# Two masks moved: the first attention's mask maximum and row scale later in VectorE's order, the second attention's mask as a 49th row of its key and query stacks

## The chip, the cores and the metric

One Trainium2 chip, one core of it. The metric is the time of one execution of the whole kernel on the device, in microseconds (us). The engines are named as in the profile: PE is TensorE's matmul side and PEld its weight load, DVE is VectorE, ACT is ScalarE, POOL is GpSimd, SP is SyncE, whose queue issues most transfers.

## The reference

The kernel runs two transformer-like layers over x (4 batches of 256 tokens, 256 wide) with a context of 1601 tokens per batch and a mask over the context for each attention. Cut to what matters:

```python
x = x + xattn0(layernorm(x), ctx, mask_b)    # 1 head, 256 wide, softmax over 1601 keys
x = x + ffn0(layernorm(x), ...)              # 16 experts, 6 per token, and 2 shared
x = x + xattn1(layernorm(x), ctx, mask_i, Wq, bq, Wk, bk, Wv, bv, Wo, bo, ...)  # 16 heads of 16
x = x + ffn1(layernorm(x), ...)              # 16 experts, 2 per token, and 1 shared

# xattn0: scores = q @ ctx.T / 16; masked keys to -1e30; softmax; times ctx;
#         the whole result is zero where a batch has no key left (valid)
# xattn1: scores = q @ k.T / 4, clipped to -50..50; masked keys to -10000, clipped again to -50;
#         softmax; times v; projected, scaled, layer norm, gamma and beta
```

## The kernel before

Tokens lie in tiles of 128, so a batch is two tiles and there are eight in all; the 1601 keys are 13 tiles of 128 (the last of 65). fp32 products are made from a rounded high part and a low remainder in three matmuls (`mm3`, lines 657 to 659): hi x hi, lo x hi and hi x lo.

**First attention and projections (stage A).** A loop over i = 0 to 7 (a batch b = i // 2 and one of its two query tiles) runs on PE, ACT and DVE, each with its own order of work written out by hand and counted semaphores between them. In each i PE makes the scores in four pieces (`scores`, two PSUM banks in turn, piece x waits for the evacuation of piece x - 2), two pieces of the key projection, the readout of the query tile before, transposes of the probabilities between two more pieces of the key projection, and four pieces of the value projection. DVE adds the mask to each score piece and takes its maximum (`row_max`), ACT makes the exponential over all 1601 keys, then rounds keys (`kev`, kh), probabilities (`pth`) and the context in natural layout (`nat_hi`, cNh), and DVE makes the low parts (`klo`, `ptl`), the values (`vev`) and adds the readout, scaled by rscale (`add_readout`). `any_key` takes the maximum of the mask row over the keys (valid), `row_scale` makes rscale = valid / sum.

In the first i of a batch (h == 0) the next batch is prepared: PE transposes its normed tokens at the end (`norm_T`), ACT rounds them (`norm_hi`, xTh) after the four context pieces (`nat_hi`), and DVE makes the remainder (`norm_lo`, xTl) as the last thing before the next `row_max`. `any_key` stands between the second and third value piece of that i. GpSimd makes the low part of the context in natural layout (cNl) and then both parts of the next batch's transposed context (cTh, cTl). The first `scores` of a batch wait for its last cTl. SP loads the context through two halves of `raw`, in the order natural pieces 2 and 3 of b, mask of b + 1 (it waits for `att_free`, which `any_key` gives), four transposed pieces of b + 1, then stores of keys.

**First router and experts (stage B)** follow, with weights split into high and low parts on DVE. In front of its expert loop DVE rounds the query weights of the second attention (`attention_weights_hi`), near its end it makes the rest (`attention_weights_lo`). The first product of the loop waits for comb_b, which comes by DMA.

**Second attention (stage C).** 16 jobs (4 batches x 4 groups of 4 heads), each over 13 key tiles: 208 steps x. The 48 stacked rows of `kst` (keys: hi, lo, hi) and `qst` (queries: hi, hi, lo) for a head, 16 rows each, give the whole three-term product in one matmul; two heads stand in partitions 0 to 47 and 64 to 111, and two more in a second column block. For each x, PE makes four score matmuls into one of three pairs of banks (`qk`), ACT one exponential of 128x1024 with scale 1/4 and the mask as a bias per key (kbias: 0 or -1e30), DVE one clip in place (`clip`, low and high bound of the exponential), and PE four heads of probabilities times values (`pv`, four steps later). PE goes in pairs of x. Between these steps stand, at fixed x, the queries of later batches (`early`) and, from the second batch on, output projection, residual, norms and routing of the batch before (`between`). Keys come from DRAM by six transfers a job (`keys`), issued three jobs ahead as soon as a slot is free; most queries are restacked by DMA in twelve transfers for each group (`queries`, `restack`), and a job's first score waits for `k_in` and, where they are restacked, `q_in`. The queries of group 0 of batches 0 and 1 come straight from PE through ACT into qst (`first_queries`), by weights whose head columns are repeated four times.

**Second router and experts (stage D)** end the kernel.

## Time and profile before

| | us |
|---|---|
| median of three runs | 754.48 |
| the three runs | 754.48, 749.64, 755.35 |
| the profiled execution's own time | 752.55 |
| its span, first to last instruction | 749.9 |

The mean granted TensorE clock of the profiled execution is 0.977 of full speed. 2.65 us of its time lie around the span. Times in the rows are counted from the span's start. Stage A reaches to about 190 us, stage B to about 411, stage C from there to about 645.

### The profile page before, as it was taken

To read this page: it belongs to the slowest core of one execution; us is meant where nothing else is said; L and a number is where in the kernel's file an instruction comes from. 1 tells how busy PE (TensorE), PEld (TensorE's weight loads), DVE (VectorE), ACT (ScalarE), POOL (GpSimd) and SP (SyncE) were. 2 spreads that over 40 slices of the span, in tenths; PEclk is the share of its full clock that TensorE was granted. 3 is DMA by queue.
4 is the path that set the end of the run, shared out by engine and by line. 5 is a ranking of instruction groups with operands and counts; after the bars stand their busy time and mean duration, and the time that the engine had idled before them with its cause. 6 is when DMAs were issued, how large, how long until landed. Compare 5 with 4: busy or idle time off the path is not lost.

```text
span 749.9 us, 14907 instructions
## 1 busy us (share of the span) xinstructions
PE 690.0 (92%) x5499; PEld 533.7 (71%) x5499; DVE 536.6 (72%) x1174; ACT 396.5 (53%) x564; POOL 174.7 (23%) x220
## 2 busy tenths in 40 slices
PE   4899999997989999999999699999999999989990
PEld 4799899997778888888887454454455454677870
DVE  5766666677576666666666788789888878775655
ACT  2633332343322222322223699999999999533550
POOL 5462625240010000000000050003203604542651
PEclk9999999999999999999999999999999999899995
DMA  7357485822728766777669959986969750474545
GB/s 250 124 182 251 136 289 152 300 93 99 225 51 290 231 221 214 240 254 234 217 211 203 129 86 188 170 128 96 214 103 197 120 68 2 149 267 133 160 132 189
DMA packets 55211, 131.14 MB, mean 175 GB/s; under 512 B 10112, under 2 KB 36096, under 8 KB 51568
## 3 DMA queue, kind: packets, MB, share of 16 engines
q1 hardware_dynamic: 51888, 122.93, 61.9%
q0 software_dynamic: 2256, 6.18, 2.4%
q10 hardware_dynamic: 1008, 1.25, 0.5%
q8 instruction: 37, 0.61, 0.4%
q14 instruction: 22, 0.18, 0.1%
HBM read 78.78 MB, written 48.79 MB: 170 GB/s over the span
## 4 chain that ended last, share of the span: by engine, by line
PE 61%; ACT 11%; issue 10%; DVE 10%; DMA 4%; POOL 2%; SPq 0%; POOLq 0%; DVEq 0%; ACTq 0%
PE ps L657 14%; PE ps L658 14%; PE ps L659 14%; ACT p L1439 7%; PE ps L1001 5%; PE ps L1189 4%; PE ps L959 3%; PE ps L1205 2%; PE ps L1023 1%; DMA raw<-in_ctxN 1%; ACT cNh L1268 1%; PE ps L741 1%; PE ps L1173 1%; DMA raw<-in_ctxT 1%; DMA comb_b<-comb_rows 1%
## 5 line engine op out<-in xcount | busy, mean ns | idle before, releaser
L1439 ACT ACTIVATE p<-ps,kbias 128x1024 f32<-128x1024 f32 (+1 forms) x208 | 211.0, 1154 | 5.8 <-PE ps L959 5.7
L1951 DVE TENSOR_SCALAR p<-p 128x1024 f32<-128x1024 f32 (+1 forms) x208 | 140.7, 689 | 25.5 <-ACT p L1439 23.8
L1001 PE MATMUL ps<-p,vsl 128*17 128x256 f32 (+1 forms) x1664 | 114.2, 383 | 2.1 <-DVE p L1951 1.0
L1344 ACT ACTIVATE hh<-h 128x512 fp32r<-128x512 f32 x50 | 31.6, 632 | 132.6 <-DVE h L1818 115.5
L959 PEld LDWEIGHTS ps<-qst,kst 48*128 48x128 f32 (+1 forms) x832 | 58.7, 182 | 60.3 <-ACT p L1439 31.4
L959 PE MATMUL ps<-qst,kst 48*128 48x256 f32 (+1 forms) x832 | 91.0, 318 | 5.7 <-DVE qst L1894 1.6
L360 POOL TENSOR_SCALAR nv<-mv 128x2 f32<-128x2 f32 x8 | 6.8, 849 | 358.1 <-DVE mv L1881 210.7
L657 PE MATMUL ps<-xTh,w_hi 128*128 128x512 f32 x200 | 79.9, 400 | 1.5 <-DVE h L1814 0.8
L658 PE MATMUL ps<-xTl,w_hi 128*128 128x512 f32 x200 | 79.3, 397 | 0.0
L659 PE MATMUL ps<-xTh,w_lo 128*128 128x512 f32 x200 | 78.9, 395 | 0.0
L1001 PEld LDWEIGHTS ps<-p,vsl 128*17 128x17 f32 (+1 forms) x1664 | 35.8, 96 | 40.2 <-issue 7.4
L1820 DVE TENSOR_TENSOR hl<-h,hh 128x512 fp32r<-128x512 f32 x50 | 34.6, 693 | 36.6 <-ACT hh L1344 36.6
L657 PE MATMUL ps<-w_hi,hh 128*128 128x256 f32 x200 | 56.9, 285 | 1.9 <-DVE hl L1820 1.7
L1814 DVE TENSOR_TENSOR h<-silu,ps 128x512 f32<-128x512 f32 x50 | 34.4, 688 | 32.9 <-PE ps L659 22.4
L659 PE MATMUL ps<-w_hi,hl 128*128 128x256 f32 x200 | 56.7, 283 | 0.0
L658 PE MATMUL ps<-w_lo,hh 128*128 128x256 f32 x200 | 56.7, 283 | 0.0
L600 POOL TENSOR_TENSOR cNl<-raw,cNh 128x1024 fp32r<-128x1024 f32 (+1 forms) x16 | 31.3, 1981 | 66.5 <-ACT cNh L1268 66.5
L657 PEld LDWEIGHTS ps<-xTh,w_hi 128*128 128x128 f32 x200 | 37.8, 189 | 9.7 <-DVE h L1814 1.7
L659 PEld LDWEIGHTS ps<-xTh,w_lo 128*128 128x128 f32 x200 | 37.5, 188 | 9.0
L658 PEld LDWEIGHTS ps<-xTl,w_hi 128*128 128x128 f32 x200 | 37.9, 189 | 6.5
L657 PEld LDWEIGHTS ps<-w_hi,hh 128*128 128x128 f32 x200 | 38.2, 191 | 5.8 <-DVE hl L1820 3.8
L1340 ACT ACTIVATE silu<-ps 128x512 f32<-128x512 f32 x50 | 29.9, 598 | 20.0 <-PE ps L659 19.0
(308 smaller groups left out, 1538.3 us busy)
## 6 DMA issues: line engine op xcount, KB each, us to landing
x_slots<-blank SPq DMA_DIRECT2D x20, 1032.0 KB, 5.9
kst<-k_hi SPq DMA_DIRECT2D x64, 200.2 KB, 8.9
w_raw<-in_w SPq DMA_DIRECT2D x25, 384.0 KB, 3.5
v_one<-vst SPq DMA_DIRECT2D x4, 1768.0 KB, 10.0
vsl<-v_one SPq DMA_DIRECT2D x4, 1768.0 KB, 17.0
kst<-k_lo SPq DMA_DIRECT2D x32, 200.2 KB, 8.9
raw<-in_ctxN SPq DMA_DIRECT2D x12, 512.0 KB, 5.7
e_w<-in_w SPq DMA_DIRECT2D x2, 3072.0 KB, 15.9
```

The costliest lines, as they stand in the source:

```text
L600: pool.tensor_tensor(cNl[:, c0:c0 + w, :], src, cNh[:, c0:c0 + w, :].bitcast(F32), ALU.subtract).then_inc(ctx_split, 1)
L657: e.matmul(o, lh, rh, start=first, stop=False, skip_group_check=True)
L658: e.matmul(o, lh, rl, start=False, stop=False, skip_group_check=True)
L659: return e.matmul(o, ll, rh, start=False, stop=last, skip_group_check=True)
L959: mm = pe.matmul(ps[0:rows, 2 * (x % RING) + t, c * SEQ:(c + 1) * SEQ], kst[r, job % KSL, c, m * P:m * P + rows], qst[r, b, 2 * g + c, :], ...
L1001: mm = pe.matmul(ps[32 * j:32 * j + VW, 6 + job % 2, 0:SEQ], vsl[0:rows, b % 2, at_:at_ + VW], p32[0:rows, x % PBUF, (2 * t + c) * SEQ:(2 ...
L1189: mm = pe.matmul(ps[:, 2 + j % 2, 0:2 * P], xbT[:, j % 2, k * P:(k + 1) * P], weights_of(j, slice(k * 2 * P, (k + 1) * 2 * P)), start=k == ...
L1344: act.activation(hh[:, half, :], h32[:, half, :], ACT.Copy).then_inc(hh_rdy, 1)
L1439: act.activation(p32[0:rows, x % PBUF, :], psf[0:rows, bank * 512:bank * 512 + 1024], ACT.Exp, scale=0.25, bias=kbias[0:rows, col:col + 1] ...
L1814: dve.tensor_tensor(h32[:, half, :], silu[:, half, :], ps[:, 5, :], ALU.mult).then_inc(mul1_rdy, 1)
L1820: dve.tensor_tensor(hl[:, half, :], h32[:, half, :], hh[:, half, :].bitcast(F32), ALU.subtract).then_inc(hl_rdy, 1)
L1951: dve.tensor_scalar(t, t, CLO, CHI, ALU.max, ALU.min).then_inc(p_clip, 1)
```

## The change

First attention: DVE does `norm_lo` of the next batch, `any_key` and the scaling of the query tile before (now `row_scale`; the reciprocal stays as `row_sum`) behind `row_max` of the next i instead of in front of it; ACT does `norm_hi` before `nat_hi` 2 and 3; SP issues the first two transposed context pieces before the next mask.

Second attention: the mask becomes row 48 of each key stack, 0 or -2**100, against a row of ones in the query stack, and the exponential has no bias. DVE makes the row for all batches in one instruction in front of the expert loop of stage B, SP stores it to DRAM (`bar_d`) and brings it by one transfer of two partitions into a slot of `kst` where the slot's batch changes. The ones come from zero weight columns with a bias of one (group 0 of batches 0 and 1) or by three transfers from `ones`.

```diff
-KR = 3 * HD
+KR = 3 * HD + 1
+BAR = -2.0 ** 100
...
+        def new_bar(job):
+            return job < KSL or job // NG != (job - KSL) // NG
+        def keys_in(job):
+            return sum(96 + 16 * new_bar(j) for j in range(job % KSL, job + 1, KSL))
...
# SP, stage B
+                    if r == 3:
+                        sp.wait_ge(bar_rdy, 1)
+                        sp.dma_start(bar_d, bar_f).then_inc(row_out, 16)
...
# SP, stage A
-            sp.dma_start(keep[:], a["keep"]).then_inc(keep_in, 16)
...
                 if b + 1 < NB:
+                    for k in range(2):
+                        load_t(b + 1, k)
                     masks_in(b + 1)
-                    for k in range(4):
+                    for k in range(2, 4):
                         load_t(b + 1, k)
...
+            sp.wait_ge(row_out, 16)
...
# keys(job)
+                if new_bar(job):
+                    sp.dma_start(kst[KR - 1:64 + KR:64, job % KSL, :, :].bitcast(F32), bar_d[job // NG:job // NG + 1, :].unsqueeze(1).broadcast_to([2, 2, MP])).then_inc(k_in[job % KSL], 16)
...
+            def ones_rows(lo, hi, done):
+                every = qst[KR - 1:64 + KR:64, :, :, :].rearrange("o b h (i n) -> o (b h i) n", n=P)
+                sp.dma_start(every[:, lo:hi, :].bitcast(F32), ones[0:2, :].bitcast(F32).unsqueeze(1).broadcast_to([2, hi - lo, P])).then_inc(done, 16)
-            for g in range(1, NG - 1):
-                queries(0, g)
+            per = NH // 2 * SEQ // P
+            sp.wait_ge(tri_rdy, 1)
+            queries(0, 1)
+            ones_rows(4, per, q_in[1])
+            queries(0, 2)
             for job in range(KSL, NJ):
                 keys(job)
                 if job == KSL:
                     queries(0, NG - 1)
+                    ones_rows(per + 4, 2 * per, q_in[NG - 1])
+                if job == 2 * KSL:
+                    ones_rows(2 * per, NB * per, q_in[NG])
...
# PE
-                    pe.wait_ge(k_in[job % KSL], 96 * (job // KSL + 1))
+                    pe.wait_ge(k_in[job % KSL], keys_in(job))
-                        pe.wait_ge(q_in[g], 16 * 3 * HG)
+                        pe.wait_ge(q_in[g], 16 * (3 * HG + (1 if g % 2 else 0)))
...
# ACT, stage A
                 if h == 0:
+                    if b + 1 < NB:
+                        norm_hi(b + 1)
                     nat_hi(b, 2)
                     nat_hi(b, 3)
-                    if b + 1 < NB:
-                        norm_hi(b + 1)
...
# ACT, stage C
-                               scale=0.25, bias=kbias[0:rows, col:col + 1]).then_inc(p_exp, 1)
+                               scale=0.25).then_inc(p_exp, 1)
...
# DVE, stage A, behind row_max(i)
                 if last:
                     next_stat(0, 3)
+                if h and b + 1 < NB:
+                    norm_lo(b + 1)
+                if h:
+                    any_key(b)
+                if i:
+                    row_scale(i - 1)
                 klo(b, h)
...
-                    dve.wait_ge(keep_in, 16)
-                    dve.tensor_scalar(kbias[:], keep[:], 0.5, -1e30, ALU.is_le, ALU.mult).then_inc(kbias_rdy, 1)
...
-                if h == 0:
-                    any_key(b)
-                row_scale(i)
+                row_sum(i)
                 for n in range(h + 2, h + 4):
                     vev(b, n)
-                if h == 0 and b + 1 < NB:
-                    norm_lo(b + 1)
...
# DVE, stage B
-                dve.wait_ge(cw_in, 16 * 8)
+                dve.wait_ge(cw_in, 16 * 9)
+                dve.tensor_scalar(bar_f, bar_i, 0.5, BAR, ALU.is_le, ALU.mult).then_inc(bar_rdy, 1)
...
                 for w, g in ((wqh, wgh), (wql, wgl)):
+                    last = g[:].bitcast(F32).rearrange("p k (h c r) -> p (k h) c r", c=64 // HD, r=HD)[:, :, 3, :]
+                    dve.memset(last, 0.0).then_inc(cw_rdy, 1)
```

A wait for d_w in front of the first `delta` comes too.

## Rows read from the trace of the kernel before

**Rows 1.** The page's part 5: costliest group (count, busy us, mean ns, idle before)

```profile
L1439 ACT ACTIVATE p<-ps,kbias 128x1024 f32<-128x1024 f32 (+1 forms) x208 | 211.0, 1154 | 5.8 <-PE ps L959 5.7
```

**Rows 2.** Busy time of a stretch: the second attention (last: clock, DMA share, GB/s)

```profile
core 0: us, PE busy (x) PEld busy (x) DVE busy (x) ACT busy (x) POOL busy (x), PEclk, DMA share, GB/s
421.00:645.00 224.00, 218.15 (x2640) 114.31 (x2637) 185.94 (x400) 217.44 (x223) 54.06 (x118) 0.99 0.72 121
```

**Rows 3.** Timeline of ACT: twelve exponentials in a row (start us, us)

```profile
436.54 12.11 ACT L1439 ACTIVATE p<-ps,kbias 128x1024 f32<-128x1024 f32 x12
```

**Rows 4.** Chain of waits in the second attention: start us, us, what

```profile
459.18 0.66 PE ps L959 x8
459.84 0.99 PE ps L1001 x16
```

**Rows 5.** Groups of ACT by shape, whole span: busy us, mean ns, idle before

```profile
L1330 ACT ACTIVATE logit<-ps 16x1024 f32<-16x1024 f32 x1 | 1.0, 1016 | 3.2 <-PE ps L659 3.2
...
L1383 ACT ACTIVATE std<-mv,eps 128x2 f32<-128x2 f32 x2 | 0.6, 295 | 1.5 <-DVE mv L1881 1.5
...
L1386 ACT ACTIVATE std<-eps 128x1 f32<-128x1 f32 x1 | 0.2, 205 | 0.0
```

**Rows 6.** Groups of PE by shape, 421.5 to 644 us: the other work

```profile
L1023 PE MATMUL ps<-wo_raw,wq_raw 128*128 128x256 f32 x24 | 6.8, 406 | 0.0
...
L657 PE MATMUL ps<-xTh,wqh 128*128 128x512 f32 x8 | 3.9, 490 | 0.1
```

**Rows 7.** Busy time of stretches: the three changes of batch

```profile
38.00:48.00 10.00, 9.08 (x62) 8.70 (x61) 6.59 (x14) 3.70 (x5) 6.86 (x6) 1.00 0.38 128
...
78.00:83.00 5.00, 3.52 (x20) 3.12 (x19) 3.72 (x7) 1.15 (x3) 3.06 (x2) 1.00 0.28 72
...
119.00:124.00 5.00, 3.54 (x20) 3.14 (x19) 3.78 (x8) 1.08 (x3) 3.05 (x2) 1.00 0.27 59
```

**Rows 8.** Chain of waits, 112 to 142 us: the third change of batch

```profile
118.23 0.33 ACT cNh L1268
...
121.34 0.45 PE ps L657
...
126.70 0.12 PE ps L657
```

**Rows 9.** Timelines of POOL and PE before scores of batches 1 and 3

```profile
53.52 1.21 POOL L613 TENSOR_TENSOR cTl<-raw,cTh 128x578 fp32r<-128x578 f32 x1
55.69 0.35 PE L657 MATMUL ps<-cTh,xTh 128*128 128x400 f32 x1
...
126.61 2.41 POOL L613 TENSOR_TENSOR cTl<-raw,cTh 128x1024 fp32r<-128x1024 f32 x1
...
135.94 1.21 POOL L613 TENSOR_TENSOR cTl<-raw,cTh 128x578 fp32r<-128x578 f32 x1
137.59 0.35 PE L657 MATMUL ps<-cTh,xTh 128*128 128x400 f32 x1
```

**Rows 10.** Timeline of DVE: mask maximum, and klo behind row_max

```profile
115.08 1.81 DVE L1571 TENSOR_REDUCE valid<-attend 128x1 f32<-128x1602 uint8 x1
...
127.81 1.18 DVE L1578 SCALAR_TENSOR_TENSOR kl<-ps,bk,kh 128x400 fp32r<-128x400 f32 x2 [2.28 <-ACT kh L1259]
...
166.65 1.18 DVE L1578 SCALAR_TENSOR_TENSOR kl<-ps,bk,kh 128x400 fp32r<-128x400 f32 x2 [1.29 <-ACT kh L1259]
```

**Rows 11.** Timelines of ACT and PE at the first change of batch

```profile
35.86 1.36 ACT L1268 ACTIVATE cNh<-raw 128x1024 fp32r<-128x1024 f32 x2 [5.77 <-DMA raw<-in_ctxN]
...
35.71 0.60 PE L692 MATMUL ps<-ident,xn 128*128 128x128 f32 x4
```

**Rows 12.** Timeline of DVE: first products of the expert loop

```profile
225.33 0.69 DVE L1814 TENSOR_TENSOR h<-silu,ps 128x512 f32<-128x512 f32 x1 [1.82 <-PE ps L659]
227.43 0.69 DVE L1818 TENSOR_TENSOR h<-h,comb_b 128x512 f32<-128x512 f32 x1 [1.41 <-DMA comb_b<-comb_rows]
```

**Rows 13.** Timelines of SP's queue and PE where job 1 begins

```profile
430.49 3.42 SPq L511 DMA_DIRECT2D qst<-ql  x4
...
436.64 0.68 PE L959 MATMUL ps<-qst,kst 48*65 48x256 f32 x8
```

More of the change, by code:

```diff
@@ L105, in build @@
         zero = sb("zero", [P, P], F32R)
-        keep = sb("keep", [P, NB * MT], I32)
-        kbias = sb("kbias", [P, NB * MT])
         with ExitStack() as s:
@@ L257, in build @@
         att_in, att_free = sem("att_in"), sem("att_free")
-        keep_in, kbias_rdy = sem("keep_in"), sem("kbias_rdy")
+        bar_rdy, row_out = sem("bar_rdy"), sem("row_out")
         neg_rdy = sem("neg_rdy")
@@ L949, in qk @@
                     elif b == 2 and g == 0:
-                        pe.wait_ge(q_in[NG], 16 * 3 * HG * NG)
+                        pe.wait_ge(q_in[NG], 16 * (3 * HG * NG + 1))
                 if x >= RING:
@@ L1433, in _ @@
                 job, m = at(x)
-                rows, col = rows_of(m), job // NG * MT + m
+                rows = rows_of(m)
                 act.wait_ge(sc_rdy, x + 1)
@@ L2006, in rows @@
                 if t == 0:
-                    dve.wait_ge(q_in[NG], 16 * 3 * HG * NG)
+                    dve.wait_ge(q_in[NG], 16 * (3 * HG * NG + 1))
                     dve.wait_ge(d_cst, 16 * 10)
```

24 lines of the change are left out of this document (15 added, 9 removed).

## The prediction

> **What bounds the kernel now.** I first read the page's groups of instructions, then busy times by stretch. The costliest group is the exponential of the second attention: 208 ACT instructions of 1154 ns, 211 us of the span [rows 1]. In the 224 us from 421 to 645 us ScalarE is busy for 217.4 us; TensorE shows 218.2 and VectorE 185.9 [rows 2]. Two engines look full, so the next view must say which one paces. In an undisturbed stretch twelve exponentials take 12.11 us; less the last one's own 1.15 us that is 0.996 us from start to start [rows 3]. The chain of waits shows TensorE's own pace where it doesn't wait: eight score matmuls (two key tiles) in 0.66 us, and their sixteen value matmuls in 0.99 us, so 1.65 us for two tiles, 0.83 for one [rows 4]. ScalarE needs 0.996, TensorE 0.83: the exponential paces, and TensorE's busy time is largely queueing. 208 tiles are 172 us of TensorE. Its other work in the stage is seen in the list of its forms: 24 output matmuls (6.8 us busy), 24 query matmuls (8 for each of three terms; about half their mean of 0.49 us apart, 5.6 us) [rows 6], and, by the code, thirty transposes of oS, thirty-two of other tiles and some short ones. I estimate 27 us in all, so TensorE's floor is about 199 us.
>
> The first attention is bound by TensorE: its stretches are full except at a change of batch, where 0.92, 1.48 and 1.46 us are idle (10.00 less 9.08, 5.00 less 3.52, 5.00 less 3.54) [rows 7]. The chain there runs from the last context transfer, through ScalarE's rounding of it (it starts at 118.23), then xTh, and on to TensorE at 121.34: xTh stands behind the two roundings in ScalarE's order, xTl behind xTh on VectorE, and the evacuation of the next scores behind xTl [rows 8]. The router and expert layer between the two is bound by TensorE, apart from one wait for comb_b [rows 12].
>
> **The change, part by part.**
>
> *Bias gone from 208 exponentials.* What does the bias operand cost? Two ACT groups differ only in it and in size: a square root with a bias tile, 128x2, takes 295 ns, an exponential without one, 128x1, takes 205 ns [rows 5]. That is 90 ns. A copy of 16x1024 without bias takes 1016 ns against the exponential's 1154, 138 ns [rows 1, 5]. Below, the overlap of neighbouring instructions might already hide all of it: 0. I take 90 ns, the like-for-like pair, off both duration and pace: 0.996 becomes 0.906, and 208 x 0.090 = 18.7 us of ScalarE time goes (bounds 0 and 29).
>
> *What is late next.* TensorE issues tiles in pairs: 1.65 us of work where ScalarE takes 1.99 now and 1.81 then. After a burst of other work it recovers 0.34 us per pair now, 0.16 then. Three score buffers hold about 2.7 us of exponentials then; less the value and score matmuls before the next tile is ready and the hand-overs, a burst of about 0.85 us can be hidden then against about 1.1 now. I went through the bursts of each batch in the order of the code with both pairs of figures (initial queries, queries at 49 and 61, the two output steps of about 1.06 us in neighbouring pairs, logits, rows_T, flips). The uncovered excess grows by 1.0 us in the start, 0.2 in the rest of batch 0, and 0.9, 1.1 and 1.1 us in the others: 4.3 us. VectorE has 38 us free in the stage [rows 2]; with 12 to 19 us less, its clips come later around the blocks of delta and router work; I give that 2 us (bounds 0 and 8). TensorE's floor caps the whole: 224 less 199 is 25 us.
>
> *A 49th row.* The score matmuls keep their count and their 256 columns. No row shows 49 partitions against 48; the nearest are 48x128 and 48x65 stationary tiles, whose matmuls keep one pace, so I take 0. The lower bound is 0 as well, as no work is removed; the upper is a rival below. The ones row of the first jobs comes out of ScalarE's existing evacuation (zero weights, bias 1). The Trainium skill (TensorEngine Tiling (Array Packing), Tiling Modes) has row tiles of 64 rows; by that, 49 rows fit like 48 and cost nothing. No row here shows it.
>
> *Its transfers.* Twelve of the 16 jobs bring one more transfer, of 25.6 KB, three of them before the stage. The queue issues it in about 0.4 us, ahead of the next keys. The sixteen DMA engines move 121 GB/s at a share of 0.72 over the stage [rows 2], so about 10.5 each when busy; if only two engines carried it, 12.8 KB each would take 1.2 us. Keys are issued some two jobs (26 tiles, 24 us) before use: hidden. The Trainium skill (DMA: Bandwidth & Descriptors, the rule "Use all 16 engines") confines a transfer whose outer dimension is 2 to two engines; at its 27 GiB/s each that would be an estimated 0.5 us, and the sum stays. Of the three transfers that fill the ones row, one isn't covered: job 1 waits on q_in[1]. Its last four query pieces are issued from 430.49 to 433.9 and the row's transfer would follow them; the tiles around job 1's first (12 and 13, eight matmuls) start at 436.64 [rows 13]. One issue and a landing of 2 to 3 us end at 436.5 to 437.5, while TensorE may come half a us earlier. I take 0.7 us (0 to 2). The other two fill rows used jobs later.
>
> Second attention: 18.7 - 4.3 - 2.0 - 0.7 = 11.7 us saved.
>
> *First attention, three changes of batch.* xTh goes ahead of the last two roundings, and xTl, the mask maximum (1.81 us) and the row scale go behind row_max. VectorE idles 2.28 us there, waiting for ScalarE's kh [rows 10]; 0.7 + 1.8 + 0.2 us makes klo about 0.4 us later, and the readout's addition behind it waits for TensorE anyway. In the last iteration three statistics stand there too and only 1.29 us is idle [rows 10]: klo moves by 0.7 us, under the same cover. So the evacuation starts when the scores are ready, and the idle 0.92, 1.48 and 1.46 us go: at most 3.9 us. But the next batch's scores wait for GpSimd's last cTl. At the first change it ends at 53.52 + 1.21 = 54.73, and the scores start at 55.69: 0.96 us to spare. At the third it ends at 137.15 and they start at 137.59: 0.44 us [rows 9]; the second is like it. This GpSimd work hangs on the context's landing, which doesn't move, so only 0.44 us is kept at each of the later two. At the first change TensorE's transposes for xTh start at 35.71 and end at 36.3, after the context was there at 35.86 [rows 11]: xTh ahead now delays the rounding, and the GpSimd chain, by about 0.9 us, so there the spare 0.96 is used up and nothing is kept. Sum 0.9 us (0 to 3.9; a delayed chain could also cost 0.5). The mask transfer now waits for att_free until behind row_max, with two context loads and the key stores queued behind it on SP. In the third change row_max ends at 127.81 - 2.28 = 125.53 now [rows 10]; 1.5 us earlier, and 2.5 us later for xTl and the maximum, VectorE frees the tile near 126.5, while the next context load has to wait for a cTl that ends at 126.61 + 2.41 = 129.02 [rows 9]: hidden. Without that cover each us late would be a us of the GpSimd chain, three times.
>
> *The rest.* The mask is made into a row in one VectorE instruction on 4 partitions (between 1 us and the maximum's 1.8), in front of a product at 225.33 that waits 1.82 us for TensorE and one at 227.43 that waits 1.41 us for comb_b [rows 12]: hidden. Two small memsets and shorter copies in the weights' preparation: about 0.1 us late on VectorE, taken as 0.1 us lost. kbias and its load go; one load, one store and one wait (row_out) come, on a queue with slack: 0.
>
> **Sum.** 11.7 + 0.9 - 0.1 = 12.5 us. The profiled execution took 752.55 us (span 749.9): 740.1. The median of the three runs is 1.9 us above it, their spread 5.7; half of that difference is added: 741.
>
> **The rivals.**
> 1. *The gain comes in full*: buffers absorb the bursts, or 0.12 us go per tile. 18.7 us or more: about 733 us. For it: TensorE's floor allows 25 us. Against: the bursts. 0.15.
> 2. *VectorE and TensorE take over as the bound*: clips held up behind delta, router and GpSimd's root leave a third of the gain, about 746 us. For it: VectorE's 185.9 us are 90% of a 206 us stage. 0.17.
> 3. *The bias was free in the pipeline*: neighbours overlap by 0.15 us already, pace stays 0.996; only the 0.9 us of the first attention is left: 751.5 us. Against: nothing in the rows shows that the operand's fetch is what overlaps. 0.12.
> 4. *Slower*: the 49th row takes from the score matmuls the pairing of the two 64-partition halves. Four take 0.33 us now; one at a time, at the 0.12 us of a full 256-column matmul [rows 8], they would take 0.48. That is 0.15 x 208 = 31 us more on TensorE: floor 230, stage 232 to 236, kernel about 761 us. It decides from about 0.1 us per tile upward. For it: no row with 49. Against: both halves end below their 64 partitions. 0.06.
>
> **How the numbers follow.** The forecast of 741 has 0.50, its own range 736 to 746. The range 733 to 749 leaves out the slower case, rival 3, and a little below. About 1% (7.5 us) is what a measurement of this kernel can tell from no change. Faster by over 1%, under 747: the forecast, rival 1 and two thirds of rival 2, 0.76. Within 1%: rival 3 and the rest, 0.18. Slower: 0.06.
>
> **What would show it.** In the second attention: exponentials of about 1.06 us, 0.906 apart in quiet stretches, a stage some 12 us shorter, more waits of ScalarE for score matmuls (5.7 us now) and fewer of TensorE for ScalarE; unchanged score pace of 0.66 us for eight. A wait for q_in[1] at the first tile of job 1. In the first attention: no idle at the third and fourth score piece, and a new wait of about 1 us for cTl before the scores of batches 1 to 3. Wrong, if the pace stays 0.996 (rival 3), if TensorE waits for clips (rival 2), or if the score matmuls space out (rival 4).

## The result and the profile after

| | us |
|---|---|
| before, median of 20 runs (range) | 752.93 (749.64 to 757.19) |
| after, median of 20 runs (range) | 748.78 (741.90 to 759.05) |
| ratio of after to before, 95% interval | 0.9945 (0.9929 to 0.9960) |
| forecast | 741.0 (733 to 749) |
| profiled execution of after: time, span, clock | 751.78, 750.0, 0.969 |

Two runs over 1.5% above the fastest of their kernel are slow and left out of the ratios, though not of medians and ranges: 759.05 us of after here, 748.68 us of e11 below.

The change saves 4.2 us (by the interval 3.0 to 5.3), a third of the forecast 12.5. The profiled execution of after is 3.0 us above its own median, so its span says nothing of the gain (750.0 against 749.9). It shows where the time lies.

The page's group of the exponential and the busy times of the second attention, after (they answer to [rows 1, 2]):

```profile
L1465 ACT ACTIVATE p<-ps 128x1024 f32<-128x1024 f32 (+1 forms) x208 | 193.3, 1052 | 12.8 <-PE ps L986 12.8
```

```profile
421.00:645.00 224.00, 215.37 (x2632) 115.70 (x2635) 185.02 (x403) 200.90 (x226) 52.88 (x117) 0.96 0.73 124
```

One exponential takes 1052 ns instead of 1154. Nine in a row, from ACT's timeline of after (start, length, as [rows 3]):

```profile
477.15 8.30 ACT L1465 ACTIVATE p<-ps 128x1024 f32<-128x1024 f32 x9
```

8.30 less the last one's 1.05 is 7.25 for eight steps: 0.906 us, just the forecast pace. The chain of waits of after has the eight score matmuls of two tiles at 0.67 us where TensorE doesn't wait, as against 0.66 in [rows 4]:

```profile
448.27 0.67 PE ps L986 x8
```

So 49 rows cost what 48 did. ScalarE is 16.5 us less busy, yet from the first exponential to the last the stage is only 2.2 us shorter, 220.1 us instead of 222.3, and it begins 3.6 us later. The exponential's own view (count, durations, first and last start), before and after:

```profile
L1439 ACT ACTIVATE p<-ps,kbias x208: 1099/1149/1282, 421.3 to 643.6; 128x1024 f32<-128x1024 f32 x96, 65x1024 f32<-65x1024 f32 x8
```

```profile
L1465 ACT ACTIVATE p<-ps x208: 1010/1043/1147, 424.9 to 645.0; 128x1024 f32<-128x1024 f32 x96, 65x1024 f32<-65x1024 f32 x8
```

**Where the late start comes from.** The stretches that had idle time in [rows 7] are full after:

```profile
78.00:83.00 5.00, 5.00 (x31) 5.00 (x30) 4.83 (x11) 0.98 (x1) 2.71 (x2) 1.00 0.37 119
119.00:124.00 5.00, 5.00 (x30) 5.00 (x29) 3.97 (x8) 1.92 (x3) 2.97 (x2) 1.00 0.12 41
...
89.00:99.00 10.00, 7.47 (x48) 7.18 (x47) 5.54 (x11) 1.99 (x5) 6.39 (x5) 0.88 0.82 250
140.00:150.00 10.00, 9.06 (x44) 9.06 (x45) 4.86 (x11) 1.25 (x1) 0.84 (x1) 0.83 0.98 339
```

The idle time is in the last two, 15 to 20 us later, and the granted clock is lower in both. PE's timeline has it in front of the first scores of batches 1, 2 and 3 (in brackets the idle time before a row):

```profile
54.90 0.43 PE L684 MATMUL ps<-cTh,xTh 128*128 128x400 f32 x1 [1.15 <-DVE vst L1623]
...
96.69 0.67 PE L684 MATMUL ps<-cTh,xTh 128*128 128x400 f32 x1 [2.52 <-issue]
...
140.94 0.67 PE L684 MATMUL ps<-cTh,xTh 128*128 128x400 f32 x1 [3.27 <-issue]
```

6.9 us of waits stand where 3.9 us were [rows 7]. "issue" and "vst" name nothing useful: by the code these scores wait for the last cTl, and the last two start 0.10 us after it ends. POOL's timeline of after beside VectorE's mask tile neg:

```profile
94.21 2.38 POOL L640 TENSOR_TENSOR cTl<-raw,cTh 128x578 fp32r<-128x578 f32 x1
...
137.72 1.83 POOL L638 CAST cTh<-raw 128x578 fp32r<-128x578 f32 x1 [0.80 <-DMA raw<-in_ctxT]
139.63 1.21 POOL L640 TENSOR_TENSOR cTl<-raw,cTh 128x578 fp32r<-128x578 f32 x1
```

```profile
94.55 0.98 DVE L1592 TENSOR_SCALAR neg<-attend 128x1602 f32<-128x1602 uint8 x1
...
138.05 0.98 DVE L1592 TENSOR_SCALAR neg<-attend 128x1602 f32<-128x1602 uint8 x1
```

A cTl of 578 columns took 1.21 us before [rows 9] and takes 2.38; a cTh took 0.67 and takes 1.83. Each has neg running inside it, and each is 1.16 or 1.17 us longer. It does not always fall out so. At the first change of after, and at the second of e3 below, the cTl beside neg kept its 1.21 us and neg took 1.52 and 1.64 us instead of 0.98. Before, neg of the second change started at 97.06, when the last cTl had ended (94.90 + 1.21 = 96.11); POOL's and DVE's timelines:

```profile
94.15 0.67 POOL L611 CAST cTh<-raw 128x578 fp32r<-128x578 f32 x1 [0.50 <-DMA raw<-in_ctxT]
94.90 1.21 POOL L613 TENSOR_TENSOR cTl<-raw,cTh 128x578 fp32r<-128x578 f32 x1
...
97.06 0.98 DVE L1566 TENSOR_SCALAR neg<-attend 128x1602 f32<-128x1602 uint8 x1
```

**Inside the second attention.** I took the starts of all 208 exponentials from ACT's timeline and summed, by stretch, what each step took above the quiet pace (0.996 us before, 0.906 without the bias). A step counts for the tile that it starts from. TensorE's bursts are its other work between tiles, delta the residual work of a batch that is done; numbers in us:

| | before | after | second part alone (e1) | no clips (e9) |
|---|---|---|---|---|
| 207 steps at the quiet pace | 206.2 | 187.5 | 187.5 | 187.5 |
| start, tiles 0 to 12 | 4.3 | 4.0 | 4.0 | 3.9 |
| TensorE's bursts | 10.2 | 17.0 | 14.4 | 14.4 |
| delta, root and rows (tiles 90 to 110, 142 to 161, 194 to 206) | 1.7 | 8.5 | 8.9 | 2.1 |
| tiles 52 to 59 | 0.0 | 3.3 | 0.8 | 0.0 |
| first to last start | 222.3 | 220.2 | 215.7 | 207.9 |

The forecast's 18.7 us of pace are there in full. 6.8 of them went in the line of delta, root and rows, and 5 in one lower clock (2.5 of the bursts, at tile 61, and 2.5 of tiles 52 to 59, both against e1): TensorE stood idle for 1.37 us, then ran 10.2 us at half the clock (0.50 of 2.4 GHz, so 1.2), from PE's timeline and the busy times:

```profile
485.19 0.65 PE L1028 MATMUL ps<-p,vsl 128*17 128x256 f32 x8 [1.37 <-DVE p L1984]
```

```profile
485.70:495.90 10.20, 10.20 (x64) 4.98 (x62) 4.52 (x10) 4.57 (x5) 0.00 (x0) 0.50 0.94 151
```

### The profile page after: what moved, and what is told of

Same layout as the page of the kernel before. It is cut to its first block, busy times and chain, and to the rows that moved or that the text cites. A ratio compares the mean times of both kernels' runs of the same rounds, so it can differ in the third digit from the quotient of the medians.

```text
span 750.0 us, 14926 instructions
## 1 busy us (share of the span) xinstructions
PE 685.2 (91%) x5499; PEld 533.6 (71%) x5499; DVE 535.0 (71%) x1176; ACT 379.8 (51%) x564; POOL 176.5 (24%) x220
## 4 chain that ended last, share of the span: by engine, by line
PE 73%; DVE 12%; POOL 5%; issue 4%; ACT 4%; DMA 2%; SPq 0%; POOLq 0%; DVEq 0%; ACTq 0%
PE ps L684 16%; PE ps L686 15%; PE ps L685 15%; PE ps L1028 9%; PE ps L986 6%; PE ps L1216 3%; DVE p L1984 2%; PE ps L1232 2%; PE ps L768 1%; ACT p L1465 1%; POOL nv L370 1%; POOL na L373 1%; PE ps L1200 1%; PE ps L1050 1%; POOL na L374 1%
## 5 line engine op out<-in xcount | busy, mean ns | idle before, releaser
L1465 ACT ACTIVATE p<-ps 128x1024 f32<-128x1024 f32 (+1 forms) x208 | 193.3, 1052 | 12.8 <-PE ps L986 12.8
L1984 DVE TENSOR_SCALAR p<-p 128x1024 f32<-128x1024 f32 (+1 forms) x208 | 139.0, 688 | 20.1 <-ACT p L1465 19.2
L1028 PE MATMUL ps<-p,vsl 128*17 128x256 f32 (+1 forms) x1664 | 118.0, 390 | 7.5 <-DVE p L1984 6.0
L370 POOL TENSOR_SCALAR nv<-mv 128x2 f32<-128x2 f32 x8 | 9.5, 1187 | 354.7 <-DVE mv L1914 208.0
L986 PEld LDWEIGHTS ps<-qst,kst 49*128 49x128 f32 (+1 forms) x832 | 57.5, 184 | 49.0 <-issue 26.6
L986 PE MATMUL ps<-qst,kst 49*128 49x256 f32 (+1 forms) x832 | 81.9, 312 | 1.3 <-DVE qst L1927 0.8
L1367 ACT ACTIVATE silu<-ps 128x512 f32<-128x512 f32 x50 | 30.0, 599 | 18.4 <-PE ps L686 17.8
## 6 DMA issues: line engine op xcount, KB each, us to landing
vsl<-v_one SPq DMA_DIRECT2D x4, 1768.0 KB, 16.5
```

The costliest lines, as they stand in the source:

```text
L986: mm = pe.matmul(ps[0:rows, 2 * (x % RING) + t, c * SEQ:(c + 1) * SEQ], kst[r, job % KSL, c, m * P:m * P + rows], qst[r, b, 2 * g + c, :], ...
L1028: mm = pe.matmul(ps[32 * j:32 * j + VW, 6 + job % 2, 0:SEQ], vsl[0:rows, b % 2, at_:at_ + VW], p32[0:rows, x % PBUF, (2 * t + c) * SEQ:(2 ...
L1367: act.activation(silu[:, half, :], ps[:, 4, :], ACT.Silu).then_inc(silu_rdy, 1)
L1465: act.activation(p32[0:rows, x % PBUF, :], psf[0:rows, bank * 512:bank * 512 + 1024], ACT.Exp, scale=0.25).then_inc(p_exp, 1)
L1984: dve.tensor_scalar(t, t, CLO, CHI, ALU.max, ALU.min).then_inc(p_clip, 1)
```

## The experiments

All times are medians against runs of the kernel before on the same chip; the ratio is that of the runs, with its 95% interval.

**e1: the second attention's part alone.** The first attention's part of the diff, on SP, ACT and DVE, is taken back (norm_lo, any_key and row_scale in front of row_max again, norm_hi behind nat_hi, the mask's load ahead of four context loads).

> The second attention's part alone (mask as a 49th row, no bias); the first attention's order is that of the kernel before. Theory A (the first attention's reordering costs time: in the profile of the changed kernel the second attention starts 3.6 us later than before instead of 0.9 us earlier): the second attention starts at 421 us again, as before, and the kernel takes about 4 us less than the changed one, 744 to 746 us. Theory B (the reordering is harmless and the late start is the scatter between executions): the time is that of the changed kernel within 1.5 us, about 749 us, or 1 us more. In the second attention the stage should still be only some 2 to 6 us shorter than before, with TensorE waiting for VectorE at the same places as in the changed kernel.

745.26 us, ratio 0.9908 (0.9877 to 0.9938). The stage runs from 422.2 to 637.9, 215.7 us long. This is Theory A: without the reordering it is 3.5 us faster than the changed kernel, though the intervals of the two ratios overlap a little (0.9938 against 0.9929).

**e2: the first attention's part alone, on the kernel before.** Just the hunks that e1 takes back.

> The first attention's part alone on the kernel before (xTh ahead of two roundings, xTl, mask maximum and row scale behind row_max, two context loads ahead of the mask). Theory A (it costs): 3 to 5 us slower than before, 756 to 758 us, TensorE waiting 1.1, 2.5 and 3.3 us before the first scores of batches 1 to 3, and a granted clock under 0.9 behind two of these waits. Theory B (harmless): 751 to 753 us. The recorded prediction had 0.9 us less than before, 752 us.

756.01 us, ratio 1.0044 (1.0022 to 1.0065): 2.6 us slower than the 753.44 of before on that chip. TensorE waits 0.61, 2.53 and 2.53 us before the first scores of batches 1 to 3. That is Theory A at the lower end of its time. The clock falls to 0.50 for 3.4 us behind the first wait of 2.53 us only; behind the second, as long, it stays at full speed. −8.2 and +2.6 make −5.6 us against the −4.2 measured: the parts add up to about 1.5 us.

**e3: a bias again, of zeros.**

```diff
-                               scale=0.25).then_inc(p_exp, 1)
+                               scale=0.25, bias=zero[0:rows, 0:1].bitcast(F32)).then_inc(p_exp, 1)
```

> The changed kernel with a bias operand again in the 208 exponentials, a column of zeros, so that only the operand differs. Theory A (the operand costs 0.09 us each and the loss elsewhere eats the gain): exponentials of about 1.15 us, 0.996 us apart; the stage 10 to 16 us longer than the changed kernel's if ScalarE paces throughout, so 759 to 765 us. Rival (most of the operand's time is hidden, because TensorE or VectorE bound the stage at 0.906): only 3 to 6 us slower than the changed kernel, 752 to 755 us, which is then also the time that the mask row is worth.

754.68 us, ratio 1.0026 (1.0004 to 1.0047). Exponentials of 1160 ns, stage 222.2 us. The operand is worth 5.9 us of the changed kernel's time, not 10 to 16: the rival, though the exponentials are 0.996 us apart again, as Theory A had it.

**e4: the bias dropped from the kernel before.**

```diff
-                               scale=0.25, bias=kbias[0:rows, col:col + 1]).then_inc(p_exp, 1)
+                               scale=0.25).then_inc(p_exp, 1)
```

> The kernel before with the exponential's bias taken away and nothing put in its place, so the second attention's mask is left out. It has no 49th row, no new transfers and no new order in the first attention: the pure worth of the operand. If the prediction's 18.7 less 4.3 and 2.0 us is right: 740 to 742 us. If the stage is bound by other engines at that pace (rival 2 of the prediction): 745 to 750 us, with the same waits of TensorE for VectorE's clips as in the changed kernel, which would then not come from the mask row or its transfers.

745.98 us, ratio 0.9912 (0.9883 to 0.9942), the same as e1. The 49th row and its transfers cost nothing that shows, and what limits the gain has nothing to do with them: e4 has the same GpSimd instruction of 3.90 us (see e5) and the same wait of TensorE of 1.76 us behind it.

**e5: VectorE lets GpSimd in,** on e1. GpSimd computes the reciprocal root of the variances in fourteen short instructions, twice a batch. As the first of the second root of a batch it adds eps to the variances (nv), on 128x2 numbers. In e1, POOL's and then DVE's timeline:

```profile
520.12 3.90 POOL L370 TENSOR_SCALAR nv<-mv 128x2 f32<-128x2 f32 x1 [4.22 <-DVE mv L2029]
```

```profile
519.95 2.46 DVE L1976 TENSOR_SCALAR p<-p 128x1024 f32<-128x1024 f32 x4
522.33 0.41 DVE L1982 COPY oS<-ps 128x256 f32<-128x256 f32 x1
522.67 1.28 DVE L1976 TENSOR_SCALAR p<-p 128x1024 f32<-128x1024 f32 x2
524.12 0.17 DVE L1989 TENSOR_SCALAR s<-ps 128x8 f32<-128x8 f32 x1 [0.17 <-PE ps L1034]
...
528.03 0.17 DVE L2036 COPY xe<-tok 128x8 f32<-128x8 f32 x1 [2.58 <-POOL rstd L378]
```

nv ends at 524.02, between 523.95 and 524.12, VectorE's first idle moment since nv began. VectorE then waits 2.58 us for the root, the clip behind that is late, and TensorE waits for the clip, at half the clock afterwards (PE's timeline and busy times of e1):

```profile
529.17 0.63 PE L1026 MATMUL ps<-p,vsl 128*17 128x256 f32 x8 [1.78 <-DVE p L1976]
```

```profile
529.90:533.30 3.40, 3.40 (x28) 1.76 (x31) 3.26 (x7) 2.36 (x3) 0.00 (x0) 0.51 1.06 195
```

The kernel before has the same lock-out, but VectorE paused sooner there: nv took 1.76 us (524.14 to 525.90), and VectorE's pause ended at 525.99. One wait on VectorE is the edit:

```diff
                         rows_mean(b)
+                        dve.wait_ge(nw, 13 * (3 + 2 * b) + 1)
```

> The second attention's part alone (745.3 us) with one more wait on VectorE: behind rows_mean of each batch it waits until GpSimd's first instruction of the second root is done. Theory (a GpSimd instruction that meets a VectorE which runs clip after clip ends only in VectorE's next idle moment: 3.90 us for that 128x2 instruction against 0.56 us elsewhere; the rows and a clip then wait 2.58 us for the root and TensorE waits behind the clip): the instruction takes about 0.6 us, VectorE's 2.58 us wait for the root in batch 0 goes to under 0.5 us at the price of about 0.8 us three times, TensorE's wait at value tile 98 (about 2 us) and the lower clock behind it go, the stage is 1.5 to 2.5 us shorter, 743 to 744 us. Rival (GpSimd's instruction is long for a cause of its own, or the three new waits cost as much): it stays near 3 us, or the stage stays within 0.5 us, 745 us or 1 us more.

POOL and DVE of e5:

```profile
518.04 0.21 POOL L370 TENSOR_SCALAR nv<-mv 128x2 f32<-128x2 f32 x1 [4.22 <-DVE mv L2029]
518.34 0.69 POOL L371 TENSOR_SCALAR rguess<-nv 128x2 int32<-128x2 int32 x1
519.11 0.52 POOL L373 TENSOR_TENSOR na<-nv,rguess 128x2 f32<-128x2 f32 x1
519.71 0.53 POOL L374 TENSOR_TENSOR na<-na,rguess 128x2 f32<-128x2 f32 x1
520.33 0.51 POOL L375 TENSOR_SCALAR na<-na 128x2 f32<-128x2 f32 x1
520.92 0.19 POOL L377 TENSOR_TENSOR rguess<-na,rguess 128x2 f32<-128x2 f32 x1
```

```profile
518.29 2.50 DVE L1976 TENSOR_SCALAR p<-p 128x1024 f32<-128x1024 f32 x4 [0.34 <-POOL nv L370]
...
524.46 0.17 DVE L2036 COPY xe<-tok 128x8 f32<-128x8 f32 x1 [0.64 <-POOL rstd L378]
```

0.21 us instead of 3.90, for a wait of 0.34; the wait for the root is 0.64, TensorE's at tile 98 is gone, the stage is 213.5 us long. That a wait on VectorE frees nv is shown. Why nv was shut out for six clips is not: the four instructions behind it start beside the same unbroken run of clips and end 0.6 us apart, one for each clip. So GpSimd does get in between two clips here, and what kept it out in e1 stays open. The root as a whole, nv to rstd, shrinks only from 7.88 to 6.38 us, as the instructions behind nv now have the clips beside them. In the table's terms e5 takes 2.5 us from the 8.9 of delta, root and rows, which leaves 6.4.

The times don't resolve it: 746.22 us (742.11 to 750.82), ratio 0.9918 (0.9886 to 0.9950), the same as e1's, where 743 to 744 us were expected. In the later batches, where nv had taken 1.13 us and not 3.90, the new wait costs 0.46 us at tiles 147 and 199 and gives back 0.3 to 0.5 us at 154 and 206.

**e6: the rows one tile later**, on e1.

```diff
-                    elif o == 45:
+                    elif o == 46:
                         rows(t)
-                    elif o == 46:
+                    elif o == 47:
                         rows(t + 1)
```

> The second attention's part alone with the two rows instructions of each batch one tile later (46 and 47 of the batch's 52 instead of 45 and 46). Theory (the spacing between the mean and the rows was made for a pace of 0.996 us and the root no longer fits into seven tiles of 0.906): the wait for the root in batch 0 falls by 0.9 us from 2.58 us, the stage is 0.5 to 1 us shorter, about 744.5 us. If the transposes of the rows, five tiles later, wait instead: no change or 0.5 us slower.

748.51 us, ratio 0.9924 (0.9904 to 0.9943), stage 216.8 us: no gain, and no loss that the interval resolves. nv still takes 3.90 us and the wait for the root is 2.31 us: the root, 0.3 us longer, ends later as well. The spacing theory fell: one tile more of room didn't help while nv was shut out.

**e7: the values of batch 1 one job earlier**, on e1.

```diff
                 if job == KSL:
+                    values(1)
                     queries(0, NG - 1)
...
-                if job == KSL + 1:
-                    values(1)
```

> The second attention's part alone with the values of batch 1 issued one job earlier. TensorE stands idle 0.8 to 1.4 us in front of value tile 53, 2.1 us after its clip had ended, in all runs without the bias and for 0.3 us with it; a granted clock of 0.5 followed it in the changed kernel's profile and 4.9 us of job 4 went. Theory (transfers crowd this stretch, 0.99 to 1.03 of the DMA engines are busy from 471 to 491 us, and TensorE's next instructions come late): with 1.8 MB gone from it the idle time shrinks below 0.5 us, the kernel is 0.5 to 1 us faster and its scatter smaller. Rival (the stall is tied to the instruction's place): 0.8 us of idle time at value tile 53 stay, 745 us.

751.22 us, ratio 0.9989 (0.9970 to 1.0008). 6 us slower than e1, where a gain of 0.5 to 1 was expected. The idle time at value tile 53 is gone, but the 1.8 MB now go ahead of job 3's query transfers, and TensorE waits for the last of these, the row of ones of q_in[3] (PE's timeline of e7). This loss is the edit's own; the run doesn't tell what the idle time at tile 53 is.

```profile
465.93 0.79 PE L983 MATMUL ps<-qst,kst 49*128 49x256 f32 x4 [6.91 <-DMA qst<-ones]
```

**e8: neg behind the last cTl, in the changed kernel.**

```diff
             def masks(b):
                 dve.wait_ge(att_in, b * 16 + 16)
+                if b:
+                    dve.wait_ge(ctx_split, raw_t(b, 3) + 1)
                 dve.tensor_scalar(neg[:], attend, 1.0, 1.6e31, ALU.subtract, ALU.mult).then_inc(neg_rdy, 1)
```

> The changed kernel with VectorE's mask tile of the next batch made behind GpSimd's last cTl instead of beside it. Theory (the mask tile, now 2.5 us earlier, runs beside GpSimd's last cTh or cTl and stretches it from 1.21 to 2.38 us or from 0.67 to 1.83, and the first scores wait for that): these instructions are back at 1.21 and 0.67 us, TensorE's waits before the first scores of batches 2 and 3 fall from 2.5 and 3.3 us to about 1.4 and 2.0, and the kernel is 1 to 3 us faster than the changed one, 746 to 748 us. Rival (the waits come from the context's arrival, not from the stretch): both waits stay within 0.5 us.

745.67 us, ratio 0.9893 (0.9863 to 0.9924): 3 to 4 us faster than the changed kernel. POOL's, DVE's and PE's timelines of e8:

```profile
94.41 1.21 POOL L640 TENSOR_TENSOR cTl<-raw,cTh 128x578 fp32r<-128x578 f32 x1
```

```profile
95.72 1.00 DVE L1594 TENSOR_SCALAR neg<-attend 128x1602 f32<-128x1602 uint8 x1 [0.83 <-POOL cTl L640]
```

```profile
55.17 0.42 PE L684 MATMUL ps<-cTh,xTh 128*128 128x400 f32 x1 [0.70 <-DVE vst L1625]
...
95.72 0.42 PE L684 MATMUL ps<-cTh,xTh 128*128 128x400 f32 x1 [1.28 <-DVE vst L1625]
...
136.71 0.42 PE L684 MATMUL ps<-cTh,xTh 128*128 128x400 f32 x1 [1.46 <-DVE vst L1625]
```

The waits are 0.70, 1.28 and 1.46 us, where [rows 7] had 0.92, 1.48 and 1.46 idle some 10 to 15 us earlier, and no lower clock follows. Undisturbed, the reordering moves the idle time and about leaves its size. VectorE's 0.83 us of waiting is covered, as the first evacuation needs the first scores.

**e9: no clips**, on e1. The kernel leaves out the bounds of the exponential.

```diff
-                dve.tensor_scalar(t, t, CLO, CHI, ALU.max, ALU.min).then_inc(p_clip, 1)
+                dve.sem_inc(p_clip, 1)
```

> The second attention's part alone with the 208 clips left out (VectorE only passes the exponential's signal on), so the bounds of the exponential are not applied. It sizes what VectorE costs in the stage, which the prediction put at 2.0 us (0 to 8) at the new pace. From the starts of the exponentials without the bias against those of before, above 0.906 and 0.996 us per tile, the three stretches around delta and the rows grew by 3.2, 2.3 and 1.8 us, 7.3 us in all, and the bursts of TensorE's other work by 4.2 us. Theory A (these three stretches are VectorE's and GpSimd's): without clips the stage goes from 215.7 to 206 to 209 us and the bursts at 22, 35, 48, 61, 115 and 167 stay as they are. Theory B (they are TensorE's bursts too, as rival 2 lets it be one of two engines): the stage stays above 212 us. TensorE's floor by the prediction was 199 us.

736.93 us (734.44 to 737.55), ratio 0.9775 (0.9740 to 0.9811). The exponential's view of e9:

```profile
L1463 ACT ACTIVATE p<-ps x208: 1010/1052/1165, 420.5 to 628.4; 128x1024 f32<-128x1024 f32 x96, 65x1024 f32<-65x1024 f32 x8
```

207.9 us; the bursts stay at 14.4 and the line of delta, root and rows falls from 8.9 to 2.1 (table above): Theory A, these stretches are VectorE's and GpSimd's. nv takes 0.21 us here with no wait added. Leaving out the clips takes away VectorE's load and its hold on GpSimd in one, so e9 doesn't split the 6.8 us between them; e5 gives 2.5 of them to nv. The idle time at tile 53 is gone too, which no theory of mine had.

**e10 to e12: both mends, and two variants.** e10 is the changed kernel with e8's wait and with e5's wait in batch 0 only; e11 moves the last cTl of each change to VectorE; e12 is e1 with e5's wait in batch 0.

```diff
# e10, e11, e12
                         rows_mean(b)
+                        if b == 0:
+                            dve.wait_ge(nw, 13 * 3 + 1)
...
# e11, DVE (GpSimd keeps k < 3)
                 if h and b + 1 < NB:
+                    kt, c0, w = TPC[3]
+                    at_ = (b + 1) % 2, kt, slice(c0, c0 + w)
+                    dve.wait_ge(tail_hi, 2 + 4 * b + 4)
+                    dve.tensor_tensor(cTl[:, at_[0], at_[1], at_[2]], raw[:, raw_t(b + 1, 3) % 2, 0:w], cTh[:, at_[0], at_[1], at_[2]].bitcast(F32), ALU.subtract).then_inc(ctx_split, 1)
                     masks(b + 1)
```

> The changed kernel with both mends: the mask tile behind GpSimd's last cTl, and VectorE's wait for GpSimd's first root instruction in batch 0. Theory (both losses are what was found and add up): the changed kernel's 748.8 us less 3.5 for the first and about 1.5 to 2 for the second, 742.5 to 744.5 us. Rival (the lower clock after the wait at value tile 53, which some executions show, takes it back): 745 to 746 us.

> As the kernel with both mends, with the last cTl of each change of batch made by VectorE instead of GpSimd. Theory (after the reordering the wait of 0.7, 1.3 and 1.5 us before the first scores of batches 1 to 3 is the length of the context chain, whose last link is GpSimd's 1.21 us cTl): VectorE takes some 0.7 us for it, each wait is about 0.5 us shorter, the kernel about 1.5 us faster than with both mends, 741 to 743 us. Rival (VectorE comes late itself, or the mask tile behind it delays the first evacuation): no gain, or 0.5 us slower.

> The second attention's part with the wait for GpSimd's first root instruction in batch 0, the first attention as before. Against the kernel with both mends it has the old order alone. Theory (mended, the reordering moves the idle time from the third score piece to the first and is worth 0.4 us: 0.70, 1.28 and 1.46 us of waits against 0.92, 1.48 and 1.47): the two are alike within 1 us, 743 to 744.5 us. Rival (the reordering is worth the 3.9 us that stood in its way): 3 us slower than the kernel with both mends.

| | median (range) | ratio (interval) |
|---|---|---|
| e10, both mends | 741.60 (739.64 to 748.67) | 0.9850 (0.9809 to 0.9891) |
| e11, and cTl on VectorE | 742.22 (737.42 to 748.68) | 0.9818 (0.9781 to 0.9855) |
| e12, old order and root mend | 742.81 (741.54 to 746.51) | 0.9855 (0.9822 to 0.9887) |

e10 beats both kernels, by 1.5% and by about 1%. e12 equals it: mended, the reordering is worth nothing that the runs can tell. The profiles of e11 and e12 both have the lower clock at tile 53, as after had: 10.2 us at 0.50 behind waits of 1.55 and 1.82 us, and job 4 takes 19.7 and 19.8 us. In e11 VectorE comes late itself (DVE's timeline):

```profile
94.45 0.42 DVE L1626 TENSOR_TENSOR vst<-ps,bv 65x256 f32<-65x256 f32 x1 [0.28 <-PE ps L687]
94.79 0.75 DVE L1736 TENSOR_TENSOR cTl<-raw,cTh 128x578 fp32r<-128x578 f32 x1
95.64 1.00 DVE L1595 TENSOR_SCALAR neg<-attend 128x1602 f32<-128x1602 uint8 x1
```

cTh was ready at 94.56; the wait before the scores is 1.23 us against e10's 1.26.

**e13 to e15: the idle time in front of value tile 53.** w1 are the weights of the second experts' shared part. e13 and e14 change e10, e15 changes e11 as e14 does.

```diff
# e13
                 if job == KSL + 2:
                     sp.wait_ge(ln_T, 8)
+                    sp.wait_ge(sc_rdy, 3 * MT + 5)
...
# e14, e15: the block moved from behind the queries to in front of keys(job)
+                if job == KSL + 2:
+                    sp.wait_ge(ln_T, 8)
+                    for k in range(NSH1):
+                        sp.dma_start(sh_raw[:, k * WC:(k + 1) * WC], a["w1"][k]).then_inc(d_in[0], 16)
                 keys(job)
```

> The kernel with both mends (741.6 us), with the w1 loads issued five tiles (4.5 us) later. Theory A (TensorE's next instructions stand behind w1 in the transfer queues, so it goes on when w1 lands): the idle time in front of value tile 53 grows from 1.1 us to 3 us or more, or stands at a later tile, and ends within 0.5 us of the landing of w1's first half, some 4 us later than now; the kernel is 1 to 4 us slower. Theory B (the idle time belongs to the tile's place, or to all traffic there): it stays at about 1 us at tile 53 and w1 lands long after it.

> The kernel with both mends, with the w1 loads issued ahead of the keys of job 5 instead of behind them, 3.4 us earlier. Theory A: w1's first half lands 2 to 3 us earlier, ahead of value tile 53 or within 0.5 us of its turn; the idle time falls from 1.1 us to under 0.4, no profile or run shows the 5 us loss in job 4, and the kernel takes 740 to 741 us with less scatter. Theory B: the idle time stays near 1 us, 741 to 742 us.

> The same earlier w1 in the kernel whose last cTl of each change is VectorE's. In the first attention this one should equal the kernel with both mends (waits of 1.2 and 1.2 us before the first scores of batches 1 and 2, as it had), since VectorE comes late to that cTl itself; in the second attention Theory A has the idle time in front of value tile 53 under 0.4 us here too and the 5 us of job 4, which its profile showed with the late w1, gone: 740 to 741 us. Theory B: 742 us, and idle time as before.

| | issue to landing, two halves | idle before tile 53 | median, ratio |
|---|---|---|---|
| e10 | 17.8, 22.6 us | 1.10 | 741.60, 0.9850 (0.9809 to 0.9891) |
| e13 | 16.6, 20.6 us | 1.11 | 741.76, 0.9840 (0.9805 to 0.9874) |
| e14 | 10.5, 15.0 us | none | 743.70, 0.9892 (0.9851 to 0.9934) |
| e15 | 10.4, 15.1 us | none | 741.29, 0.9854 (0.9817 to 0.9891) |

PE's timeline around tiles 52 and 53 (x8 is one value tile, x16 both without a pause), e10 and e14:

```profile
476.91 0.62 PE L1028 MATMUL ps<-p,vsl 128*17 128x256 f32 x8
478.63 0.63 PE L1028 MATMUL ps<-p,vsl 128*17 128x256 f32 x8 [1.10 <-DVE p L1986]
```

```profile
479.33 1.06 PE L1028 MATMUL ps<-p,vsl 128*17 128x256 f32 x16
```

In e13 the queue had been busy with the keys anyway: w1 was issued 14.4 us ahead of tile 52, where e10 had 15.6, its first half landed 2.1 us after tile 52's turn, where e10 had 2.2, and the idle time was the same. It doesn't tell the theories apart. In e14 and e15 w1 landed nearly 9 us ahead of tile 53 and the idle time is gone, which speaks for Theory A. But e9 has none either, with w1 landing 1.6 us after the tile, and e3 has 0.30 us although w1 landed 1.3 us before it. So the landing of w1 is not what the tile waits for. No gain in time shows in either; e14's runs reach from 740.74 to 750.36 us, no less scatter than e10's.

The traces hold a better sign. One of the transfer queues, q8, is of the kind "instruction" and brings blocks of 16 KB. In stage A one comes for every 231 to 293 weight loads, matmuls and waits of TensorE (259 in the mean), and no other engine's count keeps step; I take it for TensorE's. The page of after has it with packets, MB and share of the engines' time:

```profile
q8 instruction: 38, 0.62, 0.4%
```

The last block to land before value tile 53, and the start of the tile (us):

| | q8's block lands | tile 53 starts | later by | idle |
|---|---|---|---|---|
| after | 483.64 | 485.19 | 1.55 | 1.37 |
| e10 | 477.17 | 478.63 | 1.46 | 1.10 |
| e12 | 478.61 | 480.05 | 1.44 | 1.82 |
| e13 | 480.18 | 481.65 | 1.47 | 1.11 |
| before | 481.97 | 484.32 | 2.35 | none |
| e9 | 475.58 | 478.99 | 3.41 | none |
| e14 | 476.61 | 479.77 | 3.16 | none |

In all eleven profiles with idle time the tile starts 1.3 to 1.8 us behind that block, however long it had idled; in the six without, the block was there at least 2.3 us before. That fits a TensorE which waits for its own instructions, and a w1 issued earlier lets the block through earlier. No run changed the block's arrival alone, so it stays a reading of seventeen profiles, not a test.

## Why the prediction was wrong

**Right.** The operand costs 90 ns (measured 102 in the mean, 0.090 in the pace): rival 3 is false. Here the Trainium skill agrees (ScalarE: Activation LUTs, What ACT_TABLE_LOAD costs): a pointer operand adds about 93 ns. The 49th row and twelve transfers are free: rival 4 is false. The new wait for cTl before the scores came as announced, about 1 us each (0.70, 1.28 and 1.46 in e8). TensorE's bursts were sized well: 4.3 us forecast, 4.2 more in e1 than before, though 1.0 of the 4.3 was put in the start, where nothing grew. That is in part luck: the profile of before ran at a clock of 0.50 from 422.4 to 425.8, in its start, and its first slow step took 0.8 us more than e1's. The wait for q_in[1] (0.7) did not come: its ones were issued at 436.78, the tile stood at 438.97, and TensorE was busy for all of the 6 us from 436 to 442.

**The step that failed first: "with 12 to 19 us less, its clips come later around the blocks of delta and router work; I give that 2 us (bounds 0 and 8)."** The mechanism was named, its size was wrong: e1 measures 7.2 us more than before, e9 takes 6.8 of them away. I had counted VectorE's own work and its free 38 us. What the free time does not tell is where VectorE pauses. The first instruction of GpSimd's second root ended only in such a pause, at the new pace the pause in batch 0 came 2.1 us later, and VectorE then waited for the root that it had held up. e5 puts 2.5 us of the 7.2 on this. The other 4.7 lie in the same stretches and go with the clips; whether they are VectorE's own work or GpSimd's other instructions beside it, no run separates. e1's 215.7 us against the forecast 210.6 (222.3 − 11.7) are 5.1: this term's 5.2, tile 53's 0.8 and 0.9 of bursts outside the start, less 1.3 in the start (1.0 forecast, −0.3 measured) and 0.7 for q_in, which makes 4.9, the rest being rounding.

**The second: "only 0.44 us is kept at each of the later two. [...] Sum 0.9 us".** The prediction followed GpSimd's chain to its last cTl and took it as fixed by the context's landing. It followed each piece of VectorE's work that was moved, but not the one behind them: neg slid onto the chain. Measured: +2.6 us (e2) for −0.9. e8 brings 3 to 4 us back. Of those about 2.3 are the two stretched instructions. TensorE's three waits are 3.5 us shorter in e8's profile than in after's (3.44 against 6.94); what of the rest is an earlier landing of the context and what the lower clock behind longer waits is not split. And the first idle time itself was not to be had: e8's waits equal the old ones to 0.4 us in sum.

**Not in the sum at all: the clock.** In after it fell to about 0.50 for 3.4 us behind waits of TensorE of 2.52, 3.27 and 1.77 us, and for 10.2 us behind one of 1.37 (in e8 a wait of 1.37 at the same tile brought 3.4 us, in e11 and e12 1.55 and 1.82 brought 10.2); there was no drop behind 0.82 in e1, 1.10 in e10 or the second 2.53 in e2. In job 4 this cost 4.9 us (19.56 against 14.62 us from start to start of the job's exponentials in after and e1). Leaving out its run of 759.05 us, the changed kernel's lie 10.6 us apart, those of before 7.5. The scatter goes with the clock: of these nineteen the run with the lowest mean clock, 0.969, has a span of 750.0 us, the one with the highest, 0.981, has 740.0 (correlation −0.72).

**In sum** 12.5 us were forecast. Of these go 5.2 for VectorE and GpSimd, 3.5 in the first attention, 0.8 at tile 53 and 0.9 for bursts; the start and q_in give 2.0. That leaves 4.1, against 4.2 measured. So close a match is luck: the terms come from e1's profile and e2's median, the intervals of these runs are 2.3 and 1.6 us wide to either side, the medians of e1 and e2 miss the change by 1.5, and the 5 us of lower clock in after's profile are not in the sum. Rival 2, with 0.17, had the right mechanism (clips held up behind delta, router and GpSimd's root, a third of the gain left) and 746 us; the pace between these stretches stayed the exponential's, 0.906. In e1 a third of the 18.7 us, 6.6, is what the stage keeps.

## What to carry to other kernels

When a kernel's pace rises, look for the engine that lived on another's pauses: here one GpSimd instruction needed a pause of VectorE. If work moves away on VectorE, look also at what slides forward behind it, and lay both against GpSimd's timeline: here a mask instruction of 0.98 us beside the last link of GpSimd's chain cost more than the reordering could bring. A wait of 0.34 us on VectorE let a GpSimd instruction through in 0.21 us instead of 3.90 and made the stage 2.2 us shorter in the profile; the run times of e5 don't resolve that.

## What the runs showed of the hardware

A short GpSimd instruction beside back-to-back VectorE instructions can be shut out for long: 3.90 us for 128x2 numbers across six clips and a copy in e1, 1.76 us in the kernel before, each time until VectorE's next idle moment, against 0.21 in e5 and e9. It need not be: in e5 four GpSimd instructions beside the same clips took 0.51 to 0.69 us each, and one took 0.19 beside the copy. One mask instruction of 0.98 us lengthened a GpSimd instruction of 0.67 or 1.21 us by 1.17, or was itself lengthened, to 1.52 or 1.64 us. The Trainium skill (SBUF — State Buffer, Who interferes with whom) says that copy and tensor_scalar instructions can, in modes with two ports, contend with GpSimd for a shared pair of ports, and that whoever issues first holds it for the whole instruction. The traces agree in that one of the two is held up. By the recorded starts it is not always the later one: cTl of after started 0.34 us before neg and was the one lengthened. And that nv of e1 stayed out across seven VectorE instructions goes beyond what one held instruction explains.

An instruction with a zero bias column costs as much as one with real values (1160 and 1154 ns). TensorE's half clock came in two lengths, 3.4 and 10.2 us, behind a wait of the same 1.37 us, and a wait of 2.53 us brought it once and once not (e2).
